# Cross-attention with a two-of-three expert FFN on one core: router gates as row products on VectorE, experts chosen from token 0, and the b2 additions of a batch gathered in its second pair

## What is computed

```python
x = x + matmul(fake_quant(layernorm(x)), fake_quant(ctx))      # 8 bit codes, per batch
h = layernorm(x)
ratio = mean|h[:, 153:]| / (mean|h[:, :153]| + 1e-8)            # one number per batch
logits = concat(h, ratio) @ gate_w + gate_b                     # 3 experts, every token
scores = softmax(logits)
top_val, top_idx = top_k(scores, 2); top_val /= sum(top_val) + 1e-8
# the two experts of a batch are those of its token 0; the weights are each token's own
for i in range(2):
    j = top_idx[:, 0, i]                                        # one expert per batch
    out_i = act_j(h @ w1[j] + b1[j]) @ w2[j] + b2[j]            # tanh, gelu or silu
    x = x + top_val[..., i] * out_i
```

## Time and profile before

| | |
|---|---|
| time, median of 3 runs | 406.04 us (405.77 to 406.17) |
| the profiled execution | 405.39 us, of which the span is 403.6 us |
| granted clock | 0.999 of the full 2.4 GHz |
| TensorE busy | 388.8 us (96%) |
| VectorE busy | 329.3 us (82%) |
| ScalarE busy | 196.2 us (49%) |
| GpSimd busy | 57.5 us (14%) |
| DMA | 52.82 MB, 131 GB/s on average |

### The profile page before, as it was taken

How to read it: one execution, slowest core, us unless ns; L and a number is a source line. 1 busy time by engine, 2 the same in 40 slices (tenths; PEclk the granted TensorE clock), 3 DMA queues, 4 the chain that set the end, 5 groups by cost and what they waited for, 6 DMA issues and landing times.

```text
span 403.6 us, 5336 instructions
## 1 busy us (share of the span) xinstructions
PE 388.8 (96%) x1932; PEld 306.9 (76%) x1932; DVE 329.3 (82%) x512; ACT 196.2 (49%) x254; POOL 57.5 (14%) x78
## 2 busy tenths in 40 slices
PE   2998979999999999999999999999999999999996
PEld 2435736888888888888888888888888888888885
DVE  8799876488999788897899996596998865949983
ACT  3578554174347633661826455343476333425720
POOL 8748400000000003482100004000000000000000
PEclk9999999999999999999999999999999999999999
DMA  8993039523006586000000499600045870000112
GB/s 313 412 408 120 2 121 373 186 76 133 2 0 192 175 286 233 2 0 2 0 2 0 133 367 378 218 0 0 2 159 206 251 263 8 2 0 1 54 52 104
DMA packets 23325, 52.82 MB, mean 131 GB/s; under 512 B 1760, under 2 KB 1792, under 8 KB 23296
## 3 DMA queue, kind: packets, MB, share of 16 engines
q1 hardware_dynamic: 22592, 50.34, 35.0%
q0 software_dynamic: 640, 2.10, 1.5%
q10 hardware_dynamic: 64, 0.02, 0.0%
HBM read 48.26 MB, written 4.19 MB: 130 GB/s over the span
## 4 chain that ended last, share of the span: by engine, by line
PE 94%; DVE 3%; ACT 1%; DMA 1%; issue 0%; POOL 0%; POOLq 0%; DVEq 0%; ACTq 0%
PE ps L1577 43%; PE ps L1549 38%; PE ps L1343 7%; PE ps L1389 2%; PE ps L1375 2%; DMA xres<-in_x_dram 1%; PE ps L1352 1%; DVE bn L788 1%; ACT q1T L569 1%; PE ps L1410 1%; DVE xres L859 0%; PE ps L1275 0%; ACT q L526 0%; PE ps L1331 0%; PE ps L1316 0%
## 5 line engine op out<-in xcount | busy, mean ns | idle before, releaser
L634 ACT ACTIVATE w_hi<-raw 128x1024 fp32r<-128x1024 f32 x88 | 88.5, 1053 | 44.7 <-DVE raw L985 22.5
L954 DVE TENSOR_TENSOR w_lo<-raw,w_hi 128x1024 fp32r<-128x1024 f32 x88 | 103.3, 1217 | 2.2 <-ACT w_hi L634 1.9
L1577 PE MATMUL ps<-hT_hi,w_hi 128*128 128x512 f32 x256 | 99.9, 390 | 0.0
L1577 PE MATMUL ps<-hT_lo,w_hi 128*128 128x512 f32 x256 | 99.6, 389 | 0.0
L1577 PE MATMUL ps<-hT_hi,w_lo 128*128 128x512 f32 x256 | 99.6, 389 | 0.0
L1549 PE MATMUL ps<-w_hi,a_hi 128*128 128x512 f32 x224 | 87.6, 391 | 0.0
L1549 PE MATMUL ps<-w_hi,a_lo 128*128 128x512 f32 x224 | 87.2, 389 | 0.0
L1549 PE MATMUL ps<-w_lo,a_hi 128*128 128x512 f32 x224 | 87.2, 389 | 0.0
L722 ACT ACTIVATE act_f<-ps,b1T 128x512 f32<-128x512 f32 x32 | 22.0, 689 | 103.6 <-PE ps L1577 103.6
L1577 PEld LDWEIGHTS ps<-hT_hi,w_hi 128*128 128x128 f32 x256 | 48.1, 188 | 10.1 <-issue 0.2
L1577 PEld LDWEIGHTS ps<-hT_hi,w_lo 128*128 128x128 f32 x256 | 48.1, 188 | 10.0
(11 more groups left out here) (153 smaller groups left out, 375.9 us busy)
## 6 DMA issues: line engine op xcount, KB each, us to landing
raw<-in_L_ffn_w_dram SPq DMA_DIRECT2D x64, 512.0 KB, 5.5
raw<-in_ctx_dram SPq DMA_DIRECT2D x16, 512.0 KB, 11.6
xres<-in_x_dram SPq DMA_DIRECT2D x8, 512.0 KB, 9.6
b2row<-in_L_ffn_b_dram SPq DMA_DIRECT2D x4, 512.0 KB, 6.6
out_dram<-xres POOLq DMA_DIRECT2D x8, 256.0 KB, 8.0
out_dram<-xres SPq DMA_DIRECT2D x8, 256.0 KB, 2.0
small<-in_L_xattn_x_scale_dram ACTq DMA_DIRECT2D x2, 0.0 KB
small<-in_L_xattn_x_zp_dram ACTq DMA_DIRECT2D x2, 0.0 KB
```

Of the source, the lines that this page charges most:

```text
L634: nc.scalar.activation(w_hi[n % SLOTS][:, 2 * c:2 * c + 2, :], region(q)[:, 2 * c:2 * c + 2, :], ACT.Copy).then_inc(w_hi_ready, 1)
L954: V.tensor_tensor(w_lo[n % SLOTS][:, 2 * c:2 * c + 2, :], region(n % QUARTERS)[:, 2 * c:2 * c + 2, :], w_hi[n % SLOTS][:, 2 * c:2 * c + 2, ...
L1577: last = T.matmul(ps[:, G1_BANK + f % 2, :], w[q % SLOTS][:, k % TT, fs], h[:, k, :], start=n == 0, stop=n == 3 * KT - 1)
```

## The change

1. **Gates.** The 128 matmuls of `gate_product`, the copies to `lgT` and the `gate_turn` matmuls go. The gate weights are written by ACT's DMA to a buffer in HBM as three rows, and SP spreads each over all partitions (`load_gate_rows`, 3 DMAs of 512 KB, once a batch). DVE forms (x - mean) times the row, summed over the row, for each token tile and expert: 12 `gate_dot` a batch, each of 128 x 1024 f32 elements, with its products going to PSUM banks 6 and 7 as junk. `rstd` is multiplied in afterwards. Two rows lie where `act_f` blocks 4 to 7 will be written, the third in `b2row`.
2. **Experts.** TensorE computes the logits of token 0 alone (`token_logits`, 16 matmuls with 1 column as weights and 8 moving), and DVE chooses from them. The softmax and the gates follow later, in the first pair of the batch.
3. **b2.** The first pair of a batch has no b2 additions; the second has eight, at f = 0, 1 (expert of the first pair) and f = 3, 4 (its own). The b2 DMA moves to the end of SP's loads of a pair.
4. **Orders.** The lists that say which engine quantizes or copies which tile in attention change, the first loads are reordered, `b1` is turned with the gate weights, TensorE's order of attention changes, and 12 of its matmuls of batch 1 with two `add_terms` move behind block 1 of GEMM1 of pair 0.

```diff
-Q1T_BANK = [4, 5, 4, 5, 2, 3, 4, 4]
+Q1T_BANK = [4, 5, 4, 5, 2, 4, 4, 4]
...
+            sp.wait_ge(rows_out, 16)
+            sp.wait_ge(attn_done, TT)
+            load_gate_rows()
             for p in range(PAIRS):
                 sp.wait_ge(sel_ready, p + 1)
                 e = sp.value_load(expert[0:1, p:p + 1], min_val=0, max_val=NE - 1)
                 load_w1(p, 0, e)
                 load_w1(p, 1, e)
-                if p:
-                    sp.wait_ge(b2_used, TT * p)
-                sp.dma_start(b2row[:], b2[bass.ds(e, 1), :].to_broadcast([P, D])).then_inc(b2_in, 16)
                 load_w1(p, 2, e)
+                if p == TOP_K:
+                    sp.wait_ge(late_lo_ready, 4 * p)
+                    sp.wait_ge(hT_ps, B * TT)
+                    load_gate_rows()
                 load_w1(p, 3, e)
                 for q in range(4):
                     load_w2(p, q, e)
+                if p % TOP_K == 0:
+                    sp.wait_ge(dots_done, NE * TT * (p // TOP_K + 1))
+                else:
+                    sp.wait_ge(b2_used, TT * p)
+                sp.dma_start(b2row[:], b2[bass.ds(e, 1), :].to_broadcast([P, D])).then_inc(b2_in, 16)
...
+                            if f in (4, 6) and s == 0:
+                                act.wait_ge(dots_done, NE * TT * b + 2 * (f - 2))
...
+                            if f == 5 and s == 0:
+                                gate_exp(b)
...
+            def gate_dot(b, r, t):
+
+                i = b * TT + t
+                dve.wait_ge(h_stats_ready, i + 1)
+                dve.wait_ge(rows_in[r], 16 * (b + 1))
+                if r or t:
+                    dve.wait_ge(dots_done, NE * TT * b + TT * r + t)
+                elif b:
+                    dve.wait_ge(y2_done, 2 * NP * TOP_K)
+                else:
+                    dve.wait_ge(x1_ready, TT + 2)
+                junk = ps[:, JUNK_BANK:JUNK_BANK + 2, :].rearrange("p a n -> p (a n)")
+                V.scalar_tensor_tensor(out=junk, in0=xres[:, i, :], scalar=mvh[:, i, 0:1], in1=gate_row[r],
+                                       op0=ALU.subtract, op1=ALU.mult, accum_out=dot[:, r, t:t + 1]
+                                       ).then_inc(dots_done, 1)
...
+            gate_dots(0, 0)
             for p in range(PAIRS):
+                b, s = p // TOP_K, p % TOP_K
...
                         if p > 0:
                             w_lo_quarter(q + 3)
                         else:
-                            pass
+                            gate_dots(0, 1)
                     elif f == 1:
                         if p > 0:
                             t3_sum(p)
                         else:
-                            pass
+                            attn_add(1, 2)
...
                     if p == 1 and f < TT:
                         h_stats(TT + f)
-                    if f < TT:
-                        bias_add(p, f)
+                    if s:
+                        if f in (0, 1, 3, 4):
+                            for t in (f % 3 * 2, f % 3 * 2 + 1):
+                                bias_add(p - 1 if f < 3 else p, t)
+                    elif f > 1 and f < TT or p and f < TT:
+                        gate_dots(b, f)
...
+                    if s == 0 and f == TT:
+                        choose_scores(b)
+                    if s == 0 and f == TT + 2:
+                        gate_values(b)
...
                 late_lo(p, 0)
                 result(p, 0)
                 if p == 1:
+                    token_scores(1)
                     h_lo(1, 2)
                 t1_sum(p)
+                if p == 1:
+                    ratio_sums(1)
+                    router_bias(1)
+                    choose_experts(1)
                 result(p, 1)
-                if p == 1:
-                    router_bias(1)
                 w_lo_quarter(q + 7)
...
-                        last = T.matmul(ps[0:8, LOGIT_BANK, tok], gw_parts[:, k, :], h[:, k, tok],
+                        last = T.matmul(ps[0:1, LOGIT_BANK, 0:8], h[:, k, 0:1], gw_parts[:, k, :],
                                         start=n == 0, stop=n == 2 * KT - 1)
...
                     elif p == 0 and f == 2:
-                        pass
+                        codes_product(1, 2, 4)
+                        codes_product(1, 2, 5)
+                        codes_product(1, 2, 6)
+                        codes_product(1, 2, 7)
+                        add_terms(1, 2)
+                        codes_product(1, 3, 6)
+                        codes_product(1, 3, 7)
+                        add_terms(1, 3)
```

More of the change, by code:

```diff
@@ L190, in build @@
         gbias = sb("gbias", [P, NE], F32)
+        dot = sb("dot", [P, NE, TT], F32)
         lg = sb("lg", [P, NE, TT], F32)
@@ L242, in build @@
         ratio_read = sem("ratio_read")
-        logitT_ps = sem("logitT_ps")
-        logitT_ready = sem("logitT_ready")
-        logit_ps = sem("logit_ps")
+        token_ps = sem("token_ps")
+        token_read = sem("token_read")
+        gwr_ready = sem("gwr_ready")
+        rows_out = sem("rows_out")
+        rows_in = [sem(f"rows_in{e}") for e in range(NE)]
+        dots_done = sem("dots_done")
         exp_in = sem("exp_in")
@@ L325, in load_quarter, with load_gate_rows @@
                                  ).then_inc(raw_in[slot], 16)
+            def load_gate_rows():
+                for r in range(NE):
+                    sp.dma_start(gate_row[r], gate_rows[r:r + 1, :].to_broadcast([P, D])).then_inc(rows_in[r], 16)
             def load_w1(p, q, e):
@@ L893, in router_bias, with gate_dots @@
                                             op0=ALU.mult, op1=ALU.add))
+            def gate_dot(b, r, t):
[12 more added lines that the diff above has]
+                                       ).then_inc(dots_done, 1)
+            def gate_dots(b, n):
+                for i in range(3 * n, 3 * n + 3):
+                    gate_dot(b, i // TT, i % TT)
             def choose_scores(b):
-                dve.wait_ge(logit_ps, b + 1)
-                lps = ps[:, TURN_BANK[b], 0:4 * TT].rearrange("p (t e) -> p e t", e=4)
+                dve.wait_ge(dots_done, NE * TT * (b + 1))
+                dve.wait_ge(h_rstd_ready, TT * (b + 1))
+                rstd = h_rstd[:, b * TT:(b + 1) * TT]
                 for e in range(NE):
-                    last = V.tensor_scalar(sc[:, e, :], lps[:, e, :], gbias[:, e:e + 1], None, ALU.add)
+                    last = V.tensor_tensor(dot[:, e, :], dot[:, e, :], rstd, ALU.mult)
+                then(last)
+                for e in range(NE):
+                    last = V.tensor_scalar(sc[:, e, :], dot[:, e, :], gbias[:, e:e + 1], None, ALU.add)
                 then(last)
@@ L1240, in _ @@
                 w_lo_quarter(q + 9)
-                if p == 1:
-                    choose_scores(1)
-                    choose_experts(1)
                 result(p, 4)
@@ L1377, in transpose_h, with token_logits @@
                 last.then_inc(hT_ps, 1)
-            def gate_product(b, t):
-                if b == 0 and t == 0:
-                    pe.wait_ge(b1T_ready, 1)
+            def token_logits(b):
+                if b:
+                    pe.wait_ge(act_ready, TOP_K * KT)
+                else:
                     pe.wait_ge(gw_ready, 1)
-                pe.wait_ge(hT_lo_ready, 2 * (b * TT + t) + 2)
-                tok = slice(t * P, (t + 1) * P)
+                    pe.wait_ge(x1_ready, 3)
+                pe.wait_ge(hT_lo_ready, 2 * b * TT + 2)
                 n = 0
@@ L1400, in sum_abs @@
                 else:
[L1401 removed]
+                    pe.wait_ge(x1_ready, 3)
+                    if RATIO_BANK[b] == LOGIT_BANK:
+                        pe.wait_ge(token_read, 1)
                 T.matmul(ps[:, RATIO_BANK[b], 0:2 * TT], ones[:], vt[:].rearrange("p a t -> p (a t)"),
                          start=True, stop=True).then_inc(ratio_ps, 1)
[L1405 to L1412 removed]
             def turn_gate_weights():
@@ L1459, in _ @@
             codes_product(0, 2, 1)
+            codes_product(0, 1, 7)
+            codes_product(0, 3, 0)
+            codes_product(0, 3, 1)
+            add_terms(0, 0)
+            add_terms(0, 1)
             codes_product(0, 2, 2)
```

331 lines of the change are left out of this document (150 added, 181 removed).

## The result

| | before | after |
|---|---|---|
| median of the runs | 406.11 us (405.77 to 406.65, 4 runs) | 425.18 us (420.91 to 428.63, 4 runs) |
| the profiled execution | 405.39 us, span 403.6 | 427.41 us, span 425.7 |
| granted clock, mean | 0.999 | 0.972 |
| TensorE / VectorE busy | 388.8 / 329.3 us | 391.2 / 358.1 us |

The change makes the kernel slower: the ratio is 1.0388, 95% interval [1.0341, 1.0435]. The ratio sets aside the two runs of the kernel after that had the lower clock (the other two have a median of 421.9 us); since experiments 1 and 6 show that this clock is the kernel's own doing, the table gives the median over all. The forecast was 414.4 us, 401 to 420. The direction was right and the size was not.

The account below looks back on a forecast made before the run. TensorE, busy 96%, was taken to bound the kernel, with VectorE coming late. Terms -6.9 + 9.6 + 6.0 - 2.1 + 1.8 = +8.4 gave span 412.0, time 413.8, median 414.4 us; range 401 to 420.

Parts of the forecast that it names:

- Attention: Batch 0's attention: first expert known at 48.7 us, 5.8 earlier; pair 0's GEMM1 starts at 57.6, 6.9 earlier.
- F: Start of pair 0's GEMM1: 64.55 us before the change, forecast 57.6, ends 54.5 and 60.5.
- One dot: Each `gate_dot` on VectorE takes 1.46 us, from 1.2 to 2.55; 24 dots make 35 us, 12 a batch.
- rival 3: Summing costs each VectorE dot a second pass, 2.55 us a dot, giving 434 us; chance 0.06.
- Pair 0: VectorE comes late for TensorE's products 1 and 2; pair 0 grows by 3.6 + 6.0 us, ending at 149.1.
- the 0.6 for the next quarter: Pair 0's GEMM2: next quarter, behind `result`, `t1_sum` and `result`, adds 0.6 us to 5.4 of lateness.
- G: Start of pair 1's GEMM1, 146.42 us before the change; pair 0 was forecast to end at 149.1.
- Pair 1, GEMM1: Second b2 additions delay GpSimd's first h tile of batch 1; transposes start 6 us late, ends 4.0 and 9.
- Pair 1, GEMM2: Of 3.9 us removed from TensorE, 2.1 arrive; the stage takes 43.3 us against 45.4.
- S: Start of a GEMM2, here pair 1's; product 3 was forecast at 21.5 us after it.
- K: Start of pair 2, the end of pair 1's GEMM2, which was forecast to take 43.3 us.
- Pair 2: VectorE gets 16.0 us more work, 11.8 fits idle time; the pair grows by 1.8 us (0 to 4).

Follow-up runs that it names:

- experiment 1: The changed kernel with unused identity matmuls filling most of TensorE's four longest waits behind pair 0's GEMM1 start: 419.91 us, ratio 1.0357.
- experiment 6: The kernel before with four waits of different lengths put into TensorE's stream in pairs 2 and 3, nothing else: 434.25 us, ratio 1.0672.
- experiment 5: The kernel before with only the b2 additions of both pairs of a batch moved to its second pair: 415.43 us, ratio 1.0221.
- experiment 3: The changed kernel without pair 1's own b2 row (four additions, one DMA and the h tile's wait for them left out): 418.21 us, ratio 1.0306.

## Why the prediction was wrong

**Attention.** Right in kind. The first expert is known at 49.74 (forecast 48.7), F is 58.88 (57.6), 1.3 too late: TensorE's last twenty matmuls of attention begin at 54.40, where I had 53.2. Which queue lost that time was not looked for.

**One dot.** Right. The rows of after, mean 1291 and 141 ns, and 1.48 us from one start to the next, against 1.46:

```profile
L932 DVE SCALAR_TENSOR_TENSOR ps<-xres,mvh,act_f 128x1024 f32<-128x1024 f32 x16 | 20.7, 1291 | 1.3
L932 DVE DVE_READ_ACCUMULATOR ps<-xres,mvh,act_f 128x1 f32 x16 | 2.3, 141 | 0.0
```

With that, rival 3 falls. The sentence of the Trainium skill that it went with (Vector Engine (DVE) Microarchitecture Reference, section 7) doesn't hold for this form: two fp32 sources from SBUF and an accumulator, with the products going to PSUM, run at 1.26 ns an element, the plain addition at 1.25.

**Pair 0.** The work of VectorE was counted rightly: block 2 at F + 21.3 (forecast F + 21.3), `a_lo` of block 7 at F + 56.6 (56.8), and product 2 at F + 64.1 (63.6):

```profile
115.50 0.42 DVE L1043 TENSOR_TENSOR a_lo<-act_f,a_hi 128x256 fp32r<-128x256 f32 x1
...
120.96 1.22 DVE L1081 TENSOR_TENSOR a_lo<-act_f,a_hi 128x1024 fp32r<-128x1024 f32 x1
122.09 1.40 DVE L1107 SCALAR_TENSOR_TENSOR xres<-ps,gate,xres 128x512 f32<-128x512 f32 x2
```

Two details were off and cancelled, which is luck: product 2 also waits for the first `result` of product 0, in whose bank it writes (0.75 more), and the 0.6 for the next quarter didn't come. With filled waits G - F is 91.58, the forecast was 91.5. In the kernel after it is 94.30, and the 2.7 are the clock.

**Pair 1, GEMM1.** The mechanism was right and, as experiment 5 shows, enough by itself. The transposes start at G + 39.55 (39). On the way, two terms missed in opposite ways: VectorE never waited for the second b2 row (1.6 in the sum), but without that term my sum has the last addition end at G + 35.3, and it ended at 189.33 = G + 36.1; and the h tile took 3.25, not 2.3. There is also a slip in the sum itself: its terms make G + 39.2, 6.6 later than 32.6, and I put down 6.0. Then the clock: the step was +6.0, it is +7.1 with filled waits and +9.2 without.

**Pair 1, GEMM2.** Product 3 starts at S + 21.4 (21.5), by another releaser than I named: the last transposes wait 1.9 for the results of product 1. K - S is 44.3 against 43.3; 0.4 of that is the clock. `token_logits` takes 0.4 us, not 0.9, and that was worth nothing, nor was it that my S + 19.2 for TensorE comes to 19.4 by its own terms: VectorE was later.

**Pair 2.** The forecast was +1.8, it is +7.2, the largest miss of a stage: 2.7 are the clock (experiment 1), 4.5 the lateness of VectorE. The 16.0 us of new work were right, the idle time to put them in wasn't: I took 11.8, and `a_lo` of block 7 comes 6.4 later than before, so 9.6 were found. Of the time that VectorE waited for a weight 1.32 us stayed (1.5 MB of gate rows now stand ahead of these weights in the queue; that this is why is likely, but no run leaves the rows out), and 0.72 us it waited for ACT, which has just loaded tables for Exp and back, 1.28 us each. And product 2 had 2.3 to spare, not 3.0, for the same `result`.

**The sum.** By stages without the clock: F +1.3, pair 0 +0.1, pair 1 +1.1 and +0.5, pair 2 +2.7 make 5.7 above the forecast; the clock adds 7.9. That is 13.6, and the profiled execution lies 13.6 above the 413.8 that the sum gave. The 5.7 alone would have left the time at the upper end of the range: with filled waits it was 419.91. Half of the 5.7 is the idle time of VectorE in pair 2, 9.6 us found where I took 11.8, and the spare time of product 2 there.

So the step that failed is none of the five stages; it is the one between them and the sum, with 7.9 us. "The price of a wait is its length" was used without being said, though the clock of before, 0.999 throughout, came from a kernel in which TensorE never waits behind 65 us. Each of the waits that I forecast was a reason to ask what TensorE costs behind it. It is what the Trainium skill says in TensorE: Matmul & The Clock Gate (Part 1): the array's clock is halved when it has been idle and comes back once it has been busy. The windows agree (0.50 behind four waits). The same section puts what it calls the ramp penalty, the time that is lost until the clock is up, under 1% of a typical kernel's span; here, with four such stretches, it is 7.9 of 406 us, 1.9%.

**The chances.** 0.75 for slower held. The rivals that I named all doubted the lateness of VectorE or the price of a dot; none doubted TensorE itself. What remains open is which wait brings the clock down. In the traces the nine waits of 1.1 to 1.8 us behind F did not; those of 1.9 us did in five cases and not in three; one of 2.3 us did in one execution (experiment 3) and not in the two of the kernel after; all of 2.5 us and more did.

## What to carry to other kernels

A wait of TensorE isn't priced by its length: those of 3.0 us and more cost another 1.5 to 3 us each here, whether 3.3 or 8.2 long, so that a small move (4.4 us of dots) can give back more than it moves (6.7), unless the slow matmuls run into the next wait, where they cost nothing. Work taken from TensorE and given to an engine that is 82% busy was free here only in that engine's idle places; read them from its timeline, stage by stage, before the work is placed. When additions that free a buffer are moved later, look who refills the buffer: here it was GpSimd's h tile, and it alone cost 9 us.

## What was not expected of the hardware

A granted clock of 0.50 behind waits of 1.9 to 8.2 us, with 3 to 6 us of slow matmuls each, in a kernel that is 92% busy; its price of 2.5 to 2.9 us for three lengths of wait. A scalar_tensor_tensor with two fp32 sources and an accumulator at 1.29 us for 1024 columns and 0.14 for the read. Sixteen matmuls of 8 columns in 0.40 us, where sixteen of 128 columns took 0.95.
